# Gathered expert rows weighed and summed by the pair: one product of 2048 columns and three sums for 16 weighted additions and two copies

## The chip, the core and the metric

The kernel runs on one core of a Trainium2 chip. The core has TensorE (PE, matrix products), VectorE (DVE), ScalarE (ACT) and GpSimd (POOL), and SyncE (SP), which here only issues transfers. The metric is the device time of the program in microseconds.

## The reference

Two layers over `x`, 16 sequences of 256 tokens with 128 features. In each, `x` is normalized, a sequence operator gives `s`, an expert layer gives `g`, and `x` becomes `x + s * g`. The change is in the end of the first layer's expert part:

```
logits = x @ router_w                       # 32 experts
topk_w, topk_idx = top_k(softmax(logits), 4)
topk_w = topk_w / sum(topk_w)
combine = sum_k(one_hot(topk_idx) * topk_w)
eo = (silu(x @ w_gate[e]) * (x @ w_up[e])) @ w_down[e]      # for each expert e
routed = einsum('te,teh->th', combine, eo)
sh = (silu(x @ sh_gate) * (x @ sh_up)) @ sh_down * sigmoid(x @ sh_gate_w)
g = silu(routed + sh)
x = x + s * g
```

The kernel forms `routed + sh` for a token as the shared part plus four expert rows, each times its weight. The second layer has attention for `s` and a gated expert layer of 8 experts, and needs the first layer's `x`.

## The kernel before, in words

Every engine has a program of its own, and semaphores tie them together. A token tile is 128 tokens; a sequence `b` has two tiles, a pair `p` two sequences, that is four tiles, and there are 8 pairs. Sequences, pairs and steps are counted from 0.

**Routing and scatter.** DVE finds each token's four experts and a slot for each (`slot_of`), in two halves of 8 sequences. POOL sends each tile's normalized rows to its slots in HBM (`slot_rows`, line 553), 128 indirect transfers.

**Expert steps.** 48 steps (24 a half), each with 512 slots. SP loads the rows, TensorE turns them (L717), multiplies by the gate and up weights (L742), ScalarE takes silu (L971), DVE multiplies by the up part into `act` (`hidden`, L1322), TensorE turns `act` (L725) and multiplies by the down weights (L733), ScalarE copies the result out (L980) and SP stores it in `expert_rows`. TensorE runs the next step's gate and up product right after it has turned `act`.

**Gather.** When all rows of a half are stored, POOL fetches for each token its four result rows, `gath`, by indirect transfers (L567): one for each tile and rank, 8 a sequence, 16 a pair, in order of the sequences. The buffers are `onehot` and `route_tmp`, each with room for one pair and split in two sequences here, so that four sequences can be under way. A sequence's gathers wait until the one four before it is summed (`c_f`). All indirect transfers are issued by POOL, one behind another. Half 0's gathers (pairs 0 to 3) run beside the expert steps of half 1, those of half 1 (pairs 4 to 7) beside the second layer.

**Sum.** `sum_experts(b)` on DVE copies the sequence's eight weights to `f_w` (L1333), waits for its eight gathers (`g_in`), and adds row times weight in eight steps of 128 columns (`sum_step`, L1338), the two tiles taking turns. The first step of a tile starts from the shared part `sh_tok`. When both sequences of a pair are summed, ScalarE takes silu, and DVE does `mix` (x + s * g), `stats1`, `rstd1` and `norm1`. `rstd1` is 13 instructions on 4 columns, nearly each waiting for the one before. `rstd1(summed(b))` puts a step of a sum behind each of them (`link_beside`).

**Where the sums stand.** The order is written out by hand. In half 1's expert steps from step 29 on, five steps belong to a pair (`norm_step`): the even sequence is summed behind `hidden` of place 1, the odd one behind that of place 2, `mix` and `stats1` at place 3, `rstd1` at place 4, `norm1` at the next pair's place 0. So pairs 0 to 3 are done. For pairs 4 to 7 the table `NORM_AT` names the sequence of the second layer in which the pair is normalized: pair 4 in sequence 3, pair 5 in 5, pair 6 in 8, pair 7 in 10. `summed(b)` derives the sums from it: sequence 8 in b = 1, 9 in b = 2, 10 in b = 3 (beside `rstd1` of pair 4), 11 in b = 4, 12 in 6, 13 in 7, 14 in 8 (beside `rstd1`), 15 in 9.

**A sequence of the second layer on DVE**: row maximum (L1472), its negative (L1473), perhaps gates of the second router (L1399 to L1427), then a sum as above, the reciprocal (L1485), the product of hidden rows with spread gates (L1489), `finish` of the sequence before (L1460 to L1466), and the output weighed into `o_sb` (L1498). TensorE's scores of the next sequence (L855) wait for `o_sb`.

## Time and profile before

| | |
|---|---|
| median of 3 runs | 483.81 us (483.55 to 484.87) |
| profiled execution, device time | 484.73 us |
| its span | 483.0 us |
| mean granted TensorE clock | 0.936 |
| TensorE busy | 388.8 us (81%) |
| DVE busy | 331.8 us (69%), 1157 instructions |
| ScalarE busy | 261.0 us (54%) |
| POOL busy | 280.6 us (58%) |
| the chain that ended last | PE 36%, DVE 26%, POOL 13%, issue 11%, ACT 9%, DMA 4% |

The span is the profiled stretch, the device time has 1.7 us around it. The chain that ended last follows the program back from its end, at each step to what released it; its shares show which engines the time went through. POOL's share of it is the scatter near the beginning; the gathers come later and have no line among its largest.

### The profile page before, as it was taken

The numbers are of one execution on the slowest core, as the hardware profiler recorded it, in microseconds if no ns is written. First come the engines' busy times: TensorE is split into PE (matmuls) and PEld (weight loads), VectorE is DVE, ScalarE is ACT, GpSimd is POOL, SyncE is SP. The second block draws the span as 40 slices with busy tenths as digits, with TensorE's granted clock in tenths as the row PEclk, the third lists the DMA queues.
The fourth block names the chain that finished last, engine by engine and source line by source line (L and its number), as shares of the span: only waits on it lengthen the run. The fifth ranks groups of instructions, "written<-read, shape, count | busy, mean of one in ns | idle before, by whom it ended". The sixth has DMA issues, their size and how long they took to land.

```text
span 483.0 us, 8878 instructions
## 1 busy us (share of the span) xinstructions
PE 388.8 (81%) x2576; PEld 346.1 (72%) x2576; DVE 331.8 (69%) x1157; ACT 261.0 (54%) x497; POOL 280.6 (58%) x323
## 2 busy tenths in 40 slices
PE   0666887942499999985999999868888898898895
PEld 0665785932388888874999999757776776777774
DVE  6989887859446656640147869747998989885533
ACT  2250133400166666662666766467668675777772
POOL 6916777777777777754777777077777760000000
PEclk9997995977599999995999999899999999999998
DMA  6899991111435565635476666212222220100100
GB/s 182 268 358 305 313 401 65 52 49 49 157 132 181 197 202 193 185 127 178 154 212 206 205 210 202 99 54 67 82 77 72 72 87 8 43 24 22 45 12 22
DMA packets 48206, 67.26 MB, mean 139 GB/s; under 512 B 8842, under 2 KB 25635, under 8 KB 48163
## 3 DMA queue, kind: packets, MB, share of 16 engines
q1 hardware_dynamic: 39970, 49.93, 32.1%
q0 software_dynamic: 8192, 16.79, 11.4%
q8 instruction: 23, 0.38, 0.3%
q14 instruction: 21, 0.16, 0.1%
HBM read 28.93 MB, written 35.65 MB: 134 GB/s over the span
## 4 chain that ended last, share of the span: by engine, by line
PE 36%; DVE 26%; POOL 13%; issue 11%; ACT 9%; DMA 4%; SPq 1%; DVEq 0%; ACTq 0%; POOLq 0%
POOL slot_rows L553 13%; PE ps L742 12%; PE ps L733 5%; PE ps L717 4%; PE ps L725 3%; DMA rows<-slot_rows 3%; DVE trig L1338 3%; ACT L1099 2%; DVE mx L1472 2%; ACT sg L971 2%; PE ps L855 2%; DVE rows L1489 1%; PE ps L888 1%; PE ps L841 1%; DVE act L1322 1%
## 5 line engine op out<-in xcount | busy, mean ns | idle before, releaser
L553 POOL DMA_INDIRECT slot_rows<-xn_tok,slot_of x128 | 136.5, 1066 | 51.2 <-issue 38.7
L567 POOL DMA_INDIRECT onehot<-expert_rows,slot_of x64 | 61.5, 961 | 38.8 <-DMA expert_rows<-zeros 19.9
L1322 DVE TENSOR_TENSOR act<-sg,ps 128x384 f32<-128x384 f32 x48 | 26.6, 554 | 78.3 <-ACT sg L971 78.0
L567 POOL DMA_INDIRECT route_tmp<-expert_rows,slot_of x64 | 62.0, 969 | 19.5 <-issue 19.5
L733 PE MATMUL ps<-w_dn,actT 96*128 x384 | 51.0, 275 | 1.5 <-ACT actT L989 1.5
L733 PEld LDWEIGHTS ps<-w_dn,actT 96*128 96x128 f32 x384 | 46.8, 192 | 2.1 <-issue 2.0
L971 ACT ACTIVATE sg<-ps 128x384 f32<-128x384 f32 x48 | 23.6, 491 | 38.7 <-PE ps L742 38.6
L717 PE MATMUL ps<-ident,rows 128*128 128x128 f32 x192 | 32.2, 294 | 8.4 <-DMA rows<-slot_rows 5.9
L742 PE MATMUL ps<-w_gu,raw_fc 128*128 x192 | 37.9, 343 | 0.0
L980 ACT COPY zeros<-ps 128x512 f32<-128x512 f32 x48 | 28.2, 587 | 15.6 <-PE ps L733 15.2
L742 PE MATMUL ps<-w_gu,raw_pr 128*128 x192 | 35.6, 329 | 0.0
L717 PEld LDWEIGHTS ps<-ident,rows 128*128 128x128 f32 x192 | 24.4, 151 | 14.4 <-DMA rows<-slot_rows 8.8
L944 ACT ACTIVATE hs_t<-ps 128x512 f32<-128x512 f32 x16 | 9.6, 597 | 46.0 <-PE ps L650 46.0
L819 PE MATMUL ps<-prT,rows 128*128 128x128 f32 x256 | 33.3, 286 | 1.2 <-DVE raw_fc L1466 1.2
L819 PEld LDWEIGHTS ps<-prT,rows 128*128 128x128 f32 x256 | 31.9, 200 | 2.1 <-issue 1.3
L742 PEld LDWEIGHTS ps<-w_gu,raw_fc 128*128 128x128 f32 x192 | 33.0, 202 | 0.0
L725 PE MATMUL ps<-ident,act 128*96 128x128 f32 x192 | 30.4, 281 | 2.5 <-DVE act L1322 2.4
L1489 DVE TENSOR_TENSOR rows<-rows,ps 128x1024 f32<-128x1024 f32 x16 | 19.5, 1218 | 18.5 <-PE ps L882 9.8
L742 PEld LDWEIGHTS ps<-w_gu,raw_pr 128*128 128x128 f32 x192 | 30.6, 190 | 0.0
L861 PE MATMUL ps<-hs_t,fcT 128*128 128x256 f32 x128 | 30.2, 379 | 0.0
L888 PE MATMUL ps<-decay_t,hs_t 128*128 128x128 f32 x128 | 18.5, 288 | 13.7 <-ACT hs_t L1102 13.7
L989 ACT COPY actT<-ps 96x512 f32<-96x512 f32 x48 | 28.0, 583 | 2.9 <-PE ps L725 2.7
(223 smaller groups left out, 889.5 us busy)
## 6 DMA issues: line engine op xcount, KB each, us to landing
slot_rows<-zeros SPq DMA_DIRECT2D x12, 1024.0 KB, 12.4
rows<-slot_rows SPq DMA_DIRECT2D x48, 256.0 KB, 3.0
expert_rows<-zeros SPq DMA_DIRECT2D x48, 256.0 KB, 2.1
x_tok<-in_L_attn_x_dram SPq DMA_DIRECT2D x8, 256.0 KB, 5.7
slot_rows<-xn_tok,slot_of POOLq DMA_INDIRECT x128
hs_t<-xn_tok SPq DMA_DIRECT2D x16, 128.0 KB
out_dram<-raw_fc SPq DMA_DIRECT2D x16, 128.0 KB, 1.8
w_dn<-in_L_ffn_w_down_dram SPq DMA_DIRECT2D x1, 1536.0 KB
```

Of the source, the lines that this page charges most:

```text
L553: g.indirect_dma_start(out=slot_rows[r], out_offset=bass.IndirectOffsetOnAxis(ap=slot_of[:, n:n + 1], axis=0), in_=xn_tok[:, r * HT + t, : ...
L567: g.indirect_dma_start(out=gath[b % 4][:, j, :], out_offset=None, in_=expert_rows[r], in_offset=bass.IndirectOffsetOnAxis(ap=slot_of[:, n: ...
L717: mm = pe.transpose(ps[:, 0, j * P:(j + 1) * P], rows[slot][:, j * P:(j + 1) * P], ident[:])
L725: mm = pe.transpose(ps[0:I0, 5, j * P:(j + 1) * P], act[u][:, j, :], ident[:])
L733: mm = pe.matmul(ps[:, 6, j * P:(j + 1) * P], actT[u][:, j * P:(j + 1) * P], w_dn[:, bass.ds(e[j] * P, P)], start=True, stop=True)
L742: mm = pe.matmul(ps[:, 1 + 2 * u + j // 2, (j % 2) * 256:(j % 2) * 256 + 2 * I0], exT[u][:, j * P:(j + 1) * P], w_gu[:, bass.ds(e[j], 1), ...
L819: mm = pe.matmul(ps[:, 3, j * P:(j + 1) * P], hg[u][:, c, j * P:(j + 1) * P], prT[:, c, :], start=(c == 0), stop=(c == CH1 - 1))
L861: mm = pe.matmul(ps[:, 4 + c // 2, (c % 2) * SEQ:(c % 2 + 1) * SEQ], fcT[:, c, :], xn1T[u], start=True, stop=True)
L971: a.activation(sg[u][:].rearrange("p (a b) i -> p a b i", a=2), ps[:, 1 + 2 * u:3 + 2 * u, :].rearrange("p a (b i) -> p a b i", b=2)[:, :, ...
L980: a.copy(eo[slot], bank(6)).then_inc(e_out, 1)
L989: a.copy(actT[u][:], ps[0:I0, 5, :]).then_inc(e_aTs, 1)
L1322: v.tensor_tensor(act[u][:].rearrange("p (a b) i -> p a b i", a=2), sg[u][:].rearrange("p (a b) i -> p a b i", a=2), ps[:, 1 + 2 * u:3 + 2 ...
```

## The change

Buffers and gathers are counted by pairs: `gath` has two buffers of 16 rows a token tile group, `onehot` and `route_tmp`, there are two semaphores `g_in`, and a pair's 16 gathers wait once, for the pair two before it to be summed. `c_f` counts pairs. On DVE `weigh_rows(p)` waits for all 16 gathers of the pair and multiplies its 2048 columns in place by the weights, each spread over 128 columns. `sum_rows(p)` adds ranks 0 and 1 to 2 and 3 (1024 columns), then the shared part (512), then the other half (512). In the expert steps `weigh_rows` stands at place 1, `sum_rows` at place 2. In the second layer `weigh_rows` comes two sequences before the pair is normalized and `sum_rows` one before. `rstd1` no longer has steps of a sum between its instructions; `f_w`, the copies and `link_beside` are gone.

```diff
+def weighed(b):
+    return turned(b + 2) if b >= 0 else None
 def summed(b):
-    for ahead in (2, 1):
-        if b >= 0 and turned(b + ahead) is not None:
-            return 2 * turned(b + ahead) + 2 - ahead
-    return None
+    return turned(b + 1) if b >= 0 else None
...
-            for b in range(NSEQ):
-                r = b // (NSEQ // NH)
-                if b % (NSEQ // NH) == 0:
+            for p in range(FSEQ):
+                r = p // (FSEQ // NH)
+                if p % (FSEQ // NH) == 0:
                     for u in range(4):
                         pool.wait_ge(e_stored[u], 16 * (r + 1) * SG // 4)
-                if b >= 4:
-                    pool.wait_ge(c_f, b - 3)
-                for j in range(2 * TOP0):
-                    n = b * 2 * TOP0 + j
...
+                if p >= 2:
+                    pool.wait_ge(c_f, p - 1)
+                for j in range(GT):
+                    for k in range(TOP0):
+                        n = (p * GT + j) * TOP0 + k
+                        g.indirect_dma_start(
+                            out=gath[p % 2][:, j, k, :], out_offset=None, in_=expert_rows[r],
+                            in_offset=bass.IndirectOffsetOnAxis(ap=slot_of[:, n:n + 1], axis=0)).then_inc(g_in[p % 2], 16)
...
-                sc.wait_ge(c_f, 2 * p + 2)
+                sc.wait_ge(c_f, p + 1)
...
-            def sum_step(b, n, marks):
...
-            def sum_experts(b):
-                marks = []
-                for n in range(2 * TOP0):
-                    sum_step(b, n, marks)
+            def weigh_rows(p):
+                dve.wait_ge(g_in[p % 2], 16 * GT * TOP0 * (p // 2 + 1))
+                w = top_w[:, p * GT * TOP0:(p + 1) * GT * TOP0].rearrange("p (t k a) -> p t k a", t=GT, a=1)
+                link(v.tensor_tensor(gath[p % 2], gath[p % 2], w.to_broadcast([P, GT, TOP0, P]), ALU.mult))
+            def sum_rows(p):
+                g = gath[p % 2]
+                link(v.tensor_tensor(g[:, :, 0:2, :], g[:, :, 0:2, :], g[:, :, 2:4, :], ALU.add))
+                link(v.tensor_tensor(f_sb, g[:, :, 0, :], sh_tok[:, p * GT:(p + 1) * GT, :], ALU.add))
+                v.tensor_tensor(f_sb, f_sb, g[:, :, 1, :], ALU.add).then_inc(c_f, 1)
...
                 if step == 1:
-                    sum_experts(2 * q)
+                    weigh_rows(q)
                 if step == 2:
-                    sum_experts(2 * q + 1)
+                    sum_rows(q)
...
                 if turned(b) is not None:
-                    rstd1(summed(b))
-                elif summed(b) is not None:
-                    sum_experts(summed(b))
+                    rstd1()
+                if weighed(b) is not None:
+                    weigh_rows(weighed(b))
+                if summed(b) is not None:
+                    sum_rows(summed(b))
```

On DVE at pair 3, expert steps 45 to 47, the program before has (`act` is the step's product, `trig` the sum's buffer `f_sb`, `route_tmp` the gathered rows):

```order
L1322 TENSOR_TENSOR act<-sg,ps 128x384
L1333 COPY f_w<-top_w 128x8
L1338 SCALAR_TENSOR_TENSOR trig<-route_tmp,f_w,sh_tok 128x128 x2
L1338 SCALAR_TENSOR_TENSOR trig<-route_tmp,f_w,trig 128x128 x6
L1322 TENSOR_TENSOR act<-sg,ps 128x384
L1333 COPY f_w<-top_w 128x8
L1338 SCALAR_TENSOR_TENSOR trig<-route_tmp,f_w,sh_tok 128x128 x2
L1338 SCALAR_TENSOR_TENSOR trig<-route_tmp,f_w,trig 128x128 x6
L1322 TENSOR_TENSOR act<-sg,ps 128x384
```

And now:

```order
L1310 TENSOR_TENSOR act<-sg,ps 128x384
L1320 TENSOR_TENSOR route_tmp<-route_tmp,top_w 128x2048
L1310 TENSOR_TENSOR act<-sg,ps 128x384
L1324 TENSOR_TENSOR route_tmp<-route_tmp 128x4x256
L1325 TENSOR_TENSOR trig<-route_tmp,sh_tok 128x512
L1326 TENSOR_TENSOR trig<-trig,route_tmp 128x512
L1310 TENSOR_TENSOR act<-sg,ps 128x384
```

The whole pair is weighed where one sequence was summed, with one wait in front of it.

On DVE in sequence 1 of the second layer (from the second router's `top_i` on), the program before has:

```order
L1402 MAX_INDEX top_i<-top,lg 128x8 x8
L1405 TENSOR_TENSOR gd<-top 128x8
L1406 CAST g_f<-top_i 128x16
L1333 COPY f_w<-top_w 128x8
L1338 SCALAR_TENSOR_TENSOR trig<-onehot,f_w,sh_tok 128x128 x2
L1338 SCALAR_TENSOR_TENSOR trig<-onehot,f_w,trig 128x128 x6
L1485 RECIPROCAL rden<-den 128x2
L1489 TENSOR_TENSOR rows<-rows,ps 128x1024
```

And now:

```order
L1377 MAX_INDEX top_i<-top,lg 128x8 x8
L1380 TENSOR_TENSOR gd<-top 128x8
L1381 CAST g_f<-top_i 128x16
L1320 TENSOR_TENSOR onehot<-onehot,top_w 128x2048
L1462 RECIPROCAL rden<-den 128x2
L1466 TENSOR_TENSOR rows<-rows,ps 128x1024
```

The product of pair 4 stands ahead of the same reciprocal and the same product of hidden rows.

## Rows read from the trace of the kernel before

**Rows 1.** Stretches: busy us of PE, PEld, DVE, ACT, POOL; granted clock; DMA share; GB/s.

```profile
250.00:312.00 62.00, 58.91 (x444) 55.98 (x443) 49.57 (x208) 41.39 (x82) 40.27 (x42) 1.00 0.61 189
312.00:400.00 88.00, 73.53 (x476) 62.79 (x475) 71.83 (x285) 61.40 (x117) 62.12 (x64) 0.98 0.26 74
```

**Rows 2.** Timeline, sequence 1 of the second layer: start, us, instruction [idle before].

```profile
330.80 0.17 DVE L1333 COPY f_w<-top_w 128x8 f32<-128x8 f32 x1
331.07 1.03 ACT L1099 ACTIVATE rows<-ps 128x1024 f32<-128x1024 f32 x1
331.65 0.61 PE L882 MATMUL ps<-logits,expert_sel 24*128 24x256 bf16 x4
333.11 0.16 DVE L1485 RECIPROCAL rden<-den 128x2 f32<-128x2 f32 x1
333.30 1.22 DVE L1489 TENSOR_TENSOR rows<-rows,ps 128x1024 f32<-128x1024 f32 x1
```

**Rows 3.** Timeline of POOL, gathers of half 1: pair 4's first and last, pair 5's last.

```profile
314.56 0.95 POOL L567 DMA_INDIRECT onehot<-expert_rows,slot_of  x1 [11.79 <-DMA expert_rows<-zeros]
...
333.53 0.95 POOL L567 DMA_INDIRECT onehot<-expert_rows,slot_of  x1 [0.30 <-issue]
...
354.01 0.95 POOL L567 DMA_INDIRECT route_tmp<-expert_rows,slot_of  x1 [0.30 <-issue]
```

**Rows 4.** Timeline of POOL, half 0: the last gathers of pairs 2 and 3.

```profile
281.35 0.95 POOL L567 DMA_INDIRECT onehot<-expert_rows,slot_of  x1 [0.30 <-issue]
...
301.68 1.10 POOL L567 DMA_INDIRECT route_tmp<-expert_rows,slot_of  x1 [0.30 <-issue]
```

**Rows 5.** Timeline of DVE, pair 2's first copy and pair 3's sums.

```profile
282.75 0.17 DVE L1333 COPY f_w<-top_w 128x8 f32<-128x8 f32 x1
...
300.62 0.17 DVE L1333 COPY f_w<-top_w 128x8 f32<-128x8 f32 x1
...
303.70 0.55 DVE L1322 TENSOR_TENSOR act<-sg,ps 128x384 f32<-128x384 f32 x1 [0.69 <-ACT sg L971]
...
304.38 0.61 DVE L1338 SCALAR_TENSOR_TENSOR trig<-route_tmp,f_w,sh_tok 128x128 f32<-128x128 f32 x2
```

**Rows 6.** Groups of DVE instructions by form, 240 to 483 us: busy us, mean ns | idle before.

```profile
L1489 DVE TENSOR_TENSOR rows<-rows,ps 128x1024 f32<-128x1024 f32 x16 | 19.5, 1218 | 18.5 <-PE ps L882 9.8 <-ACT rows L1099 8.6
...
L1361 DVE TENSOR_TENSOR trig<-out_cs,xnT 128x512 f32<-128x512 f32 x4 | 2.8, 693 | 0.0
```

**Rows 7.** Timeline of DVE and POOL, two places where they overlap.

```profile
73.75 1.22 DVE L1279 TENSOR_TENSOR_SCAN rec<-decay,rec 128x512 f32<-128x512 f32 x1
73.81 1.94 POOL L553 DMA_INDIRECT slot_rows<-xn_tok,slot_of  x1 [0.30 <-issue]
...
347.04 0.69 DVE L1361 TENSOR_TENSOR trig<-trig,xnT 128x512 f32<-128x512 f32 x1
...
347.39 1.15 POOL L567 DMA_INDIRECT route_tmp<-expert_rows,slot_of  x1 [0.30 <-issue]
```

**Rows 8.** Timeline of DVE, `rstd1` alone (ahead of L1386) and with sums between (sequence 3).

```profile
311.00 0.17 DVE L1379 TENSOR_SCALAR v<-mv 128x4 f32<-128x4 f32 x1
...
313.45 1.11 DVE L1386 TENSOR_SCALAR rec<-x_tok,mv,r 128x128 f32<-128x128 f32 x4
...
350.61 0.17 DVE L1379 TENSOR_SCALAR v<-mv 128x4 f32<-128x4 f32 x1
...
354.63 0.17 DVE L1485 RECIPROCAL rden<-den 128x2 f32<-128x2 f32 x1
```

**Rows 9.** Busy by stretch as in rows 1; timeline of TensorE; chain that ended last.

```profile
220.00:223.00 3.00, 0.49 (x3) 0.49 (x4) 0.00 (x0) 0.00 (x0) 0.85 (x1) 0.50 0.88 307
...
222.51 1.12 PE L717 MATMUL ps<-ident,rows 128*128 128x128 f32 x4 [3.86 <-DMA rows<-slot_rows]
...
225.48 2.57 PE ps L742 x8
230.01 1.30 PE ps L742 x8
```

More of the change, by code:

```diff
@@ L242, in build @@
         f_act = out_cs[:].rearrange("p c (a d) -> p (c a) d", d=P)
-        f_w = [sb(f"f_w{u}", [P, 2 * TOP0]) for u in range(2)]
         st1 = sb("st1", [P, 4, 6])
@@ L331, in build @@
         e_stored = [sem(f"e_stored{u}") for u in range(4)]
-        g_in = [sem(f"g_in{u}") for u in range(4)]
+        g_in = [sem(f"g_in{u}") for u in range(2)]
         xr_in = [sem(f"xr_in{u}") for u in range(2)]
@@ L1058, in tanh_f @@
             def tanh_f(p):
-                sc.wait_ge(c_f, 2 * p + 2)
+                sc.wait_ge(c_f, p + 1)
                 a.activation(f_act, f_sb, ACT.Tanh, scale=0.5).then_inc(c_fact, 1)
@@ L1373, in stats1, with rstd1 @@
                 link(last)
[L1375 to L1380 removed]
+            def rstd1():
+                link(v.tensor_scalar(v1[:], mv1[:, :, 1], EPS, None, ALU.add))
+                rsqrt_steps(nc, link, r1[:], v1[:], t1[:])
             def norm1(p):
```

36 lines of the change are left out of this document (2 added, 34 removed).

## The prediction

> **What bounds the kernel now.** I read the page first, then busy time by stretch, then the gathers and the DVE rows around them. The chain that ended last is spread over four engines, with DVE's line 1338, the sums to be replaced, among its pieces. By stretch two regimes stand out. From 250 to 312 us, the last expert steps, TensorE is busy 58.91 of 62 us: each step begins as the one before it ends, and DVE only has to deliver `act` in time. From 312 to 400 us, attention with pairs 4 to 7 between, DVE has 71.83 of 88 us and TensorE 73.53 with pauses [rows 1]. There the chain is DVE's. In sequence 1 the gate product at 333.30 starts 0.2 us after the reciprocal, though its inputs were ready with the gelu at 332.10 and the spread gates at 332.26 [rows 2]. So DVE is already 1.0 us late there, and anything added in front of 333.11 moves the rest.
>
> The quantity that decides is when gathered rows are there. Gathers start 1.26 us apart: pair 4's first at 314.56, its sixteenth at 333.53, pair 5's sixteenth at 354.01 [rows 3]. In the first half pair 2's last one starts at 281.35, pair 3's at 301.68 [rows 4]. The landing is not shown, but bounded: pair 3's last gather leaves POOL at 302.78 and DVE uses its row at 304.38, at once after its copy [rows 4, 5]. So it is between 0 and 1.6 us; I take 1.5, because nearest to the only row.
>
> By the Trainium skill ("DMA: Bandwidth & Descriptors", Anatomy of one DMA — SWDGE (gpsimd) path) a DMA of this kind has a fixed cost of about 2.0 us. Counted from the start of the 1.10 us gather that would be 0.9 us behind its end, which agrees with the bound; each wait below would be 0.6 us shorter by it.
>
> **The change part by part.**
>
> *The arithmetic.* Removed per pair: two copies and sixteen steps of 128 columns. In sequence 1 a copy and eight steps take 330.80 to 333.11, 2.31 us [rows 2], so 4.6 us a pair. Added: products of 512 columns take 693 ns and of 1024 columns 1218 ns [rows 6], 1.025 ns a column and 168 ns fixed. The trace has none of 2048 columns; by the line it is 2.27 us, at least 1.22 (the 1024 row) and, at that row twice over, at most 2.44. I take 2.3. The three sums have 1024, 512 and 512 columns: 1.22 + 0.69 + 0.69 and two links of 0.03, 2.7 us. A pair needs 5.0 us in place of 4.6: the instructions are fewer, the columns the same, and a product and an addition that were one pass are now two.
>
> *The wait for the pair.* `weigh_rows` stands where the even sequence was summed, but waits for 16 gathers and not for 8. The eight more take 10 us of POOL. The places:
> - Pair 3: DVE comes to it at 300.62; its rows are there at 302.78 + 1.5 = 304.3. It waits 3.7, the product ends at 306.6, and the next `act` product, at 303.70 before [rows 5], is 2.9 late. TensorE's transposes of `act`, the next gate/up group and with them every later step are queued behind it, and the last stores, on which POOL's second series of gathers waits, move too.
> - Pair 2: wanted at 282.75, there at 282.30 + 1.5 = 283.8; a wait of 1.0 of which 0.7 is idle time that DVE had.
> - Pair 4, in sequence 1: wanted at 330.80, there at 333.53 + 0.95 + 1.5 = 336.0. Wait 5.2, all of it late, since the gate product, the finish, `o_sb` and TensorE's next scores are queued behind it.
> - Pairs 0, 1, 6 and 7: their rows are there first, by the same pitch.
> If the landing were 0 or 1.6, the waits of pairs 3 and 4 would be 1.5 shorter or 0.1 longer each.
>
> *POOL held up by wide DVE instructions.* A POOL issue that starts within a DVE instruction with both inputs in SBUF lasts until that ends. At 73.81, just inside the scan of 73.75 to 74.97, it takes 1.94 us; at 347.39, inside the product of 347.04 to 347.73, 1.15 [rows 7]; clear of such instructions gathers take 0.95 [rows 3]. The hold ends some 0.15 us before the DVE instruction does. The old steps hold for 0.13 us or so each. The product holds for 2.1, which is longer than the pitch of the gathers: one always starts inside it, on average 0.63 in, and is 1.5 late (least 0.9, most 2.1). The sums, holding 1.07, 0.53 and 0.53, add 0.5 + 0.1 + 0.1 on average. That is 2.2 a pair, less 0.1 for the old steps. Since pair 1's gathers run under pair 0's sums and so on, pair 2's rows come 4.2 later (288.0) and pair 3's 6.3 later (310.6). The product then ends at 312.9 and the step that began at 303.70 is 9.2 late; with the least hold it is 2.9 + 3 x 0.9 = 5.6. I take 8: nearer to the average, and a little under it because pair 0's product starts shortly before a gather ends. It takes the place of the 2.9 above.
>
> The Trainium skill ("SBUF — State Buffer", Who interferes with whom) says that a DVE instruction with two SBUF inputs contends with a GpSimd instruction that reads SBUF, whichever issued first keeping the port, but infers that descriptor generation isn't held by `tensor_tensor`. By the first rule the sum is mine; by the inference it is that of the first rival. The issues at 73.81 and 347.39 stand for the first.
>
> *Attention's sum.* Pair 4's wait 5.2. Its sums in sequence 2, in the path like those of sequence 1: 2.7 for 2.3, +0.4. Pair 5 in sequence 3: before, the steps filled the links of the reciprocal root, the two together taking 350.61 to 354.63, 4.0 us; alone the root takes 311.00 to 313.45, 2.45 us [rows 8]. With the product that is 4.75: +0.7. Pair 5's last gather, held by pair 4's product and sums (2.2), lands at 354.96 + 2.2 + 1.5 = 358.7, and DVE wants it at 350.61 + 5.2 + 0.4 + 2.45 = 358.7: +0.3, between 0 and 0.7. Pair 6 +0.4 in sequence 7, pair 7 +0.7 in sequence 8. The sums in sequences 4 and 9 stand beside ScalarE's table loads and gelu; nothing (0.4 each if that cover is gone). 5.2 + 0.4 + 0.7 + 0.3 + 0.4 + 0.7 = 7.7.
>
> *TensorE's clock.* After the pause of 3.86 us before 222.5 the granted clock was 0.50, the lower of its levels, 1.2 of 2.4 GHz, and the gate/up group took 2.57 us in place of 1.30 [rows 9]. The three waits above 3 us leave TensorE idle as long. A spell costs about 2 us in the expert steps (that group and its neighbours), next to nothing where DVE is the limit: between 0 and 6, I take 2.
>
> *POOL's own waits* for `c_f` now name a whole pair. Pair 6's gathers need pair 4 summed, one sequence (10 us) after 333.11 and 5.6 late, at 349, and follow pair 5's last at 354.01 [rows 3] anyway: nothing. The same holds for pair 7.
>
> The sum, against the profiled execution: 483.0 span and 1.7 around it are 484.73; + 8 + 7.7 + 2 = 502.4. Its 484.73 lie 0.9 above the median of 483.81, so the median should be 501.5.
>
> **The rivals.**
> 1. *Only the waits*, POOL not held. For: the issues of [rows 3] all show 0.95 us. Against: the issues at 73.81 and 347.39. Then 2.9 + 7.4 + 1 of clock = 11.3, and the median is 495.1.
> 2. *One wait covered.* Should DVE's wait in the expert steps lie beside a row load or a store that ends as late, or the landing be near 0, 5 to 8 us are left: 489 to 492. Against: `act` is what TensorE waits for at each of these steps.
> 3. *Not slower: both waits covered.* If DVE had slack behind sequence 1 of as much as 5.2 us, the wait would only take the place of idle time further on (from that slack on it decides), and the 4.6 for 5.0 us of work would be lost in it too: 484. For it speaks that DVE is idle 16 of 88 us from 312 to 400. Against: the row at 333.30 has its slack used up.
> 4. *More than counted*: every product holding for its longest and a clock spell at each wait: 9.2 + 8.5 + 6, the median at 507.5 or above.
>
> **How the numbers follow.** A difference of 0.3%, 1.5 us, is what a measurement of this kernel can tell from none. The forecast 0.54, its own range 497 to 506; rival 1 0.23; rival 2 0.08; rival 3 0.06; rival 4 0.09. The range of 8 in 10 takes in the forecast and rival 1 and leaves out rivals 2 and 3 and most of 4: 492.5 to 507.5. Slower: all but rival 3, 0.94. Rival 3 is split: 0.03 within 0.3%, 0.03 faster.
>
> **What would show it.** In the profile after: DVE idle in front of the product of 2048 columns, ended by a gather, for about 5 us each at pairs 2, 3 and 4, nothing at pairs 0, 6 and 7. The product about 2.3 us. Some POOL issue of 2 to 3 us under each product, and pair 3's last gather near 309 in place of 301.7. The second series of gathers starting near 323 in place of 314.6. Sequences 10 to 15 as long as before. I am wrong if the wait at pair 4 is under 4 us, if the product is far from 2.3, or if no POOL issue under a product is longer than 1.4 us.

## The result: 4.2% slower, and the profile after

| | before | after |
|---|---|---|
| median | 483.73 us (483.55 to 484.87, 4 runs) | 503.51 us (502.87 to 506.49, 4 runs) |
| profiled execution, its span | 484.73, 483.0 us | 504.15, 502.4 us |
| mean granted TensorE clock | 0.936 | 0.921 |
| DVE busy | 331.8 us, 1157 instructions | 334.3 us, 1045 instructions |
| POOL busy | 280.6 us | 292.7 us |

The ratio is 1.0416, with a 95% interval from 1.037 to 1.0462. The forecast was 501.5 us, within 492.5 to 507.5. The two profiled spans differ by 19.4 us.

The page of the kernel after shows where the reader has to look. Its section 4 is the chain that ended last, first by engine, then by engine, tile and line.

```profile
POOL 29%; DVE 22%; PE 20%; issue 15%; ACT 7%; DMA 6%; SPq 1%; DVEq 0%; POOLq 0%; ACTq 0%
```

Before, the chain was 36% TensorE, 26% DVE and 13% POOL, and POOL's 13% were the scatter alone. Now the gathers `onehot L555` and `route_tmp L555` have 9% and 7% of it: TensorE has lost its place to them.

By stretch, busy time of PE, PEld, DVE, ACT, POOL, then granted clock, DMA share and GB/s, the kernel after, as in [rows 1]:

```profile
250.00:312.00 62.00, 54.53 (x389) 52.12 (x388) 40.64 (x134) 36.05 (x71) 47.49 (x43) 0.92 0.58 176
312.00:400.00 88.00, 69.83 (x427) 59.78 (x426) 65.45 (x220) 53.05 (x103) 56.38 (x54) 0.92 0.24 68
```

In the same 62 us TensorE gets 4.4 us less done and DVE 8.9, while POOL is busy 7.2 us longer with as many instructions (43 for 42). Longer busy time for the same count is a sign of instructions held up, not of more work. I call it a hold when a POOL issue lasts longer than its usual 0.94 us because a DVE instruction is running.

The waits of DVE in the kernel after: who waits, for what, total us, times, the longest.

```profile
DVE onehot L1320 <- DMA onehot<-expert_rows,slot_of: 9.8, 2, 6.0
DVE route_tmp L1320 <- DMA route_tmp<-expert_rows,slot_of: 4.1, 2, 2.4
```

L1320 is the product of 2048 columns. Of its eight instances four wait for gathers, 13.9 us together. The timeline (start, us, instruction, idle before) gives their places, pairs 1 to 4: ahead of each product the pair's sixteenth gather, behind the first two also the POOL issue that runs beside them:

```profile
264.50 0.94 POOL L555 DMA_INDIRECT route_tmp<-expert_rows,slot_of  x1 [0.30 <-issue]
...
267.49 2.29 DVE L1320 TENSOR_TENSOR route_tmp<-route_tmp,top_w 128x2048 f32<-128x2048 f32 x1 [2.40 <-DMA route_tmp<-expert_rows,slot_of]
268.24 2.36 POOL L555 DMA_INDIRECT onehot<-expert_rows,slot_of  x1 [0.30 <-issue]
...
286.87 0.94 POOL L555 DMA_INDIRECT onehot<-expert_rows,slot_of  x1 [0.30 <-issue]
...
289.89 2.29 DVE L1320 TENSOR_TENSOR onehot<-onehot,top_w 128x2048 f32<-128x2048 f32 x1 [5.95 <-DMA onehot<-expert_rows,slot_of]
290.62 2.39 POOL L555 DMA_INDIRECT route_tmp<-expert_rows,slot_of  x1 [0.30 <-issue]
292.22 0.55 DVE L1310 TENSOR_TENSOR act<-sg,ps 128x384 f32<-128x384 f32 x1
...
309.35 0.94 POOL L555 DMA_INDIRECT route_tmp<-expert_rows,slot_of  x1 [0.30 <-issue]
...
312.09 2.29 DVE L1320 TENSOR_TENSOR route_tmp<-route_tmp,top_w 128x2048 f32<-128x2048 f32 x1 [1.69 <-DMA route_tmp<-expert_rows,slot_of]
314.42 0.55 DVE L1310 TENSOR_TENSOR act<-sg,ps 128x384 f32<-128x384 f32 x1
...
344.42 0.94 POOL L555 DMA_INDIRECT onehot<-expert_rows,slot_of  x1 [0.30 <-issue]
...
347.05 2.29 DVE L1320 TENSOR_TENSOR onehot<-onehot,top_w 128x2048 f32<-128x2048 f32 x1 [3.82 <-DMA onehot<-expert_rows,slot_of]
349.38 0.17 DVE L1462 RECIPROCAL rden<-den 128x2 f32<-128x2 f32 x1
```

The sixteenth gathers are those at 264.50, 286.87, 309.35 and 344.42. Those of pairs 2 and 3, at 281.35 and 301.68 before [rows 4], are 5.5 and 7.7 later. The `act` product at 303.70 before [rows 5] stands at 314.42. The reciprocal of sequence 1, at 333.11 before [rows 2], stands at 349.38, 16.3 later. POOL's second series starts 11.1 later than in [rows 3]:

```profile
325.70 0.94 POOL L555 DMA_INDIRECT onehot<-expert_rows,slot_of  x1 [15.41 <-DMA expert_rows<-zeros]
```

**Two stages.** For everything that follows I divide the program at one instruction that every kernel has: the row maximum `mx` of a sequence of the second layer. Its first (sequence 0) ends the expert stage, its last (sequence 15) the attention stage. Before, they start at 315.91 and 468.09; after, at 325.55 and 487.56. So 9.6 of the us were lost in the expert stage and 9.8 in attention. In attention the delay is 12.5 us at sequence 1, 17.2 at sequence 2, 18.6 at sequence 4, and 19.5 from sequence 9 to the end.

The delay at the last `act` product, just ahead of the first `mx`, is 10.7 (318.42 for 307.71), and so 1.1 more than at `mx`. That 1.1 us is a clock spell of the kernel before: its TensorE ran at the low level there, and takes 8.2 us from the last `act` product to `mx`; the kernel after ran that stretch at 1.00, in 7.1.

```profile
312.00:314.00 2.00, 2.00 (x7) 1.64 (x7) 1.72 (x11) 0.28 (x1) 0.00 (x0) 0.50 0.35 131
```

I call a spell a stretch of a few us at the low granted clock. Which spells an execution has differs from kernel to kernel, and each one that isn't followed by a wait for something else is worth 1 to 1.5 us in these figures.

### The profile page after: what moved, and what is told of

Read it like the earlier page. It is cut to its first block, busy times and chain, and to the rows that moved or that the text cites. A ratio compares the mean times of both kernels' runs of the same rounds, so it can differ in the third digit from the quotient of the medians.

```text
span 502.4 us, 8755 instructions
## 1 busy us (share of the span) xinstructions
PE 397.3 (79%) x2576; PEld 353.2 (70%) x2576; DVE 334.3 (67%) x1045; ACT 261.1 (52%) x497; POOL 292.7 (58%) x323
## 4 chain that ended last, share of the span: by engine, by line
POOL 29%; DVE 22%; PE 20%; issue 15%; ACT 7%; DMA 6%; SPq 1%; DVEq 0%; POOLq 0%; ACTq 0%
POOL slot_rows L540 13%; POOL onehot L555 9%; POOL route_tmp L555 7%; PE ps L730 5%; DMA rows<-slot_rows 3%; PE ps L721 2%; PE ps L849 2%; PE ps L705 2%; ACT L1087 2%; PE ps L843 1%; PE ps L807 1%; DVE rows L1466 1%; DVE route_tmp L1320 1%; DVE mx L1447 1%; PE ps L876 1%
## 5 line engine op out<-in xcount | busy, mean ns | idle before, releaser
L555 POOL DMA_INDIRECT onehot<-expert_rows,slot_of x64 | 65.6, 1025 | 42.8 <-DMA expert_rows<-zeros 24.0
L555 POOL DMA_INDIRECT route_tmp<-expert_rows,slot_of x64 | 70.3, 1098 | 21.3 <-issue 21.3
L730 PE MATMUL ps<-w_gu,raw_fc 128*128 x192 | 39.0, 350 | 0.0
L977 ACT COPY actT<-ps 96x512 f32<-96x512 f32 x48 | 28.0, 583 | 11.7 <-PE ps L713 11.6
L849 PE MATMUL ps<-hs_t,fcT 128*128 128x256 f32 x128 | 32.6, 400 | 0.0
L1466 DVE TENSOR_TENSOR rows<-rows,ps 128x1024 f32<-128x1024 f32 x16 | 19.5, 1218 | 18.5 <-PE ps L870 9.8
L713 PEld LDWEIGHTS ps<-ident,act 128*96 128x96 f32 x192 | 20.0, 127 | 14.3 <-DVE act L1310 13.0
## 6 DMA issues: line engine op xcount, KB each, us to landing
w_dn<-in_L_ffn_w_down_dram SPq DMA_DIRECT2D x1, 1536.0 KB, 16.3
```

The lines of the kernel that those rows point to most:

```text
L555: g.indirect_dma_start(out=gath[p % 2][:, j, k, :], out_offset=None, in_=expert_rows[r], in_offset=bass.IndirectOffsetOnAxis(ap=slot_of[:, ...
L713: mm = pe.transpose(ps[0:I0, 5, j * P:(j + 1) * P], act[u][:, j, :], ident[:])
L730: mm = pe.matmul(ps[:, 1 + 2 * u + j // 2, (j % 2) * 256:(j % 2) * 256 + 2 * I0], exT[u][:, j * P:(j + 1) * P], w_gu[:, bass.ds(e[j], 1), ...
L849: mm = pe.matmul(ps[:, 4 + c // 2, (c % 2) * SEQ:(c % 2 + 1) * SEQ], fcT[:, c, :], xn1T[u], start=True, stop=True)
L977: a.copy(actT[u][:], ps[0:I0, 5, :]).then_inc(e_aTs, 1)
L1466: v.tensor_tensor(hg[u], hg[u], ps[:, 0:2, :].rearrange("p a (b n) -> p (a b) n", b=2), ALU.mult).then_inc(d_hs, 1)
```

## The experiments

### Six runs beside a disturbance

The first six runs settled nothing about time. In those two sessions every engine paused now and then, the longest time in each run for 37 to 43 us, for nothing that the profile could name, and the kernel before itself took 740 us (medians 739.68 in the first four, 743.65 in the last two). A difference of 10 us can't be read beside that. The record gives chip 0 for the first session and chip 5 for the second; five of the six later runs were made on chip 5 too, and there the kernel before then took 484 to 485 us. The kernels are those of the sections below, where their edits stand, and they were run again later with the same expectations. These six, with what was on record for them:

The waits alone, measured 740.12 us, ratio 1.0042 (0.9993 to 1.009); and again, 744.46, ratio 0.9932 (0.9866 to 0.9997):

> The kernel before with one thing added: the even sequence's sum also waits for the odd one's eight gathers. Narrow steps, copies, order and POOL's waits as before. Theory: the waits without the holds. Landing 2.0 us after the issue ends: pair 2 about 1 us late, pair 3 about 3.4 us, pair 4 waits 5.5 us, and 2 to 4 us of lower clock behind them: 495 to 498; the POOL issues stay at 0.95 us. Rival (the wide instructions cost nothing of their own): as the changed kernel, 502 to 504. Rival (the wait is small, the holds are all): 485 to 488.

> The kernel before with one thing added: the even sequence's sum also waits for the odd one's eight gathers. Narrow steps, copies, order and POOL's waits as before. Theory: the waits without the holds. Landing 2.0 us after the issue ends: pair 2 about 1 us late, pair 3 about 3.4 us, pair 4 waits 5.5 us, and 2 to 4 us of lower clock behind them: 495 to 498; the POOL issues stay at 0.95 us. Rival (the wide instructions cost nothing of their own): as the changed kernel, 502 to 504. Rival (the wait is small, the holds are all): 485 to 488.

The product in eight pieces, 745.32 us, ratio 1.0102:

> The changed kernel with the product of 2048 columns cut in eight of 256, back to back, no links between. Theory (POOL waits for the one DVE instruction that it meets): holds under a product are at most 0.3 us, 0.25 a pair on average in place of 1.5; the longest POOL issue under a product is under 1.3 us; the product takes 2.7 us for 2.3; pair 3's rows come about 3.7 us earlier: 498 to 501. Rival (DVE keeps POOL out as long as its two-input instructions follow each other): POOL issues of 2 us and more remain, 503 to 505.

Half waits, 743.93 us, ratio 1.0083 (1.004 to 1.0127):

> The changed kernel, with four semaphores for the gathers, so that DVE waits for the even sequence's eight gathers where the product stood and for the odd one's where the sums stand; the product is two of 1024 columns. Theory (pair wait, POOL held up, clock): the wait of sequence 1 of the second layer goes, since pair 4's second eight are asked for 10 us later; in the expert steps holds of 0.5 and 0.5 for the products and 0.7 for the sums, 1.7 us a pair, still put pair 3's last gather near 307.8, landed near 309.8, so that DVE waits there about 5 us for the odd half; the work at that place is 3.9 us in place of 2.4. Median 491 to 496. Rival (the wait for the whole pair is all): 484 to 487.

TensorE kept busy, 744.80 us, ratio 1.0105 (1.0016 to 1.0193); and again, 745.53, ratio 1.0035:

> The changed kernel with small unused TensorE products (128x64, bf16, into columns that are overwritten later) where TensorE would be idle: 80 and 30 in the waits of pairs 2 and 3, 36 in sequence 0 and 80 ahead of the scores of sequence 2 of the second layer. Theory (part of the loss is the lower granted clock after the waits): the granted clock stays at 1.00 from 286 to 360 us, the step that took 6.5 us behind pair 2's wait takes 4.0 again, and the time falls by 4 to 7 us, to 497 to 500. Rival (the lower clock costs nothing where DVE is waited for): 502 to 505.

> The changed kernel with small unused TensorE products (128x64, bf16, into columns that are overwritten later) where TensorE would be idle: 80 and 30 in the waits of pairs 2 and 3, 36 in sequence 0 and 80 ahead of the scores of sequence 2 of the second layer. Theory (part of the loss is the lower granted clock after the waits): the granted clock stays at 1.00 from 286 to 360 us, the step that took 6.5 us behind pair 2's wait takes 4.0 again, and the time falls by 4 to 7 us, to 497 to 500. Rival (the lower clock costs nothing where DVE is waited for): 502 to 505.

One thing could be read in them, since it is a single instruction's length: with the whole product POOL's longest gather issue was 2.48 and 2.49 us, with the product in pieces 1.42.

### Only the waits

The kernel before, in which an even sequence's sum also waits for the gathers of the odd one. Nothing is added on DVE, and no instruction is wide.

```diff
                     dve.wait_ge(g_in[b % 4], 16 * 2 * TOP0 * (b // 4 + 1))
+                    if b % 2 == 0:
+                        dve.wait_ge(g_in[b % 4 + 1], 16 * 2 * TOP0 * (b // 4 + 1))
```

> The kernel before with one thing added: the even sequence's sum also waits for the odd one's eight gathers. Narrow steps, copies, order and POOL's waits as before. Theory: the waits without the holds. Landing 2.0 us after the issue ends: pair 2 about 1 us late, pair 3 about 3.4 us, pair 4 waits 5.5 us, and 2 to 4 us of lower clock behind them: 495 to 498; the POOL issues stay at 0.95 us. Rival (the wide instructions cost nothing of their own): as the changed kernel, 502 to 504. Rival (the wait is small, the holds are all): 485 to 488.

Measured: 494.81 us against 485.35 for the kernel before in the same session, ratio 1.0173 (1.0099 to 1.0247), that is 8.4 us, or 9.5 by the medians. That is 0.2 below the expected 495 to 498, and far from both rivals. DVE's rows in front of the sum (L1340 here) at pairs 2, 3 and 4:

```profile
286.17 0.67 DVE L1340 SCALAR_TENSOR_TENSOR trig<-onehot,f_w,sh_tok 128x128 f32<-128x128 f32 x2 [3.98 <-DMA onehot<-expert_rows,slot_of]
...
305.13 0.61 DVE L1340 SCALAR_TENSOR_TENSOR trig<-route_tmp,f_w,sh_tok 128x128 f32<-128x128 f32 x2 [0.52 <-DMA route_tmp<-expert_rows,slot_of]
...
340.84 0.61 DVE L1340 SCALAR_TENSOR_TENSOR trig<-onehot,f_w,sh_tok 128x128 f32<-128x128 f32 x2 [3.77 <-DMA onehot<-expert_rows,slot_of]
```

and its gathers by group (count, busy us, mean ns, idle before), first of this kernel, then of the kernel after:

```profile
L567 POOL DMA_INDIRECT route_tmp<-expert_rows,slot_of x64 | 61.8, 965 | 19.5 <-issue 19.5
L567 POOL DMA_INDIRECT onehot<-expert_rows,slot_of x64 | 61.7, 965 | 45.2 <-DMA expert_rows<-zeros 26.3 <-issue 18.9
```

```profile
L555 POOL DMA_INDIRECT onehot<-expert_rows,slot_of x64 | 65.6, 1025 | 42.8 <-DMA expert_rows<-zeros 24.0 <-issue 18.9
L555 POOL DMA_INDIRECT route_tmp<-expert_rows,slot_of x64 | 70.3, 1098 | 21.3 <-issue 21.3
```

With the wait alone a gather takes 965 ns as ever. With the change the 128 gathers take 12.4 us more of POOL (135.9 for 123.5). The wait by itself costs about half of the whole loss. Where it does: the first `mx` is 3.5 us late for 9.6 with the whole change, and the rest of the expert stage's loss needs the wide instructions. Attention takes 161.0 us in place of 152.2. Not all of these 8.9 us are the wait's: 1.5 of them come in sequence 4 (11.9 us for 10.4 in the kernels before and after), where this execution's granted clock was 0.55 from 376 to 379 and those two have no spell.

```profile
370.05 0.68 DVE L1474 TENSOR_REDUCE mx<-ps 128x2 f32<-128x512 f32 x1
...
381.96 0.69 DVE L1474 TENSOR_REDUCE mx<-ps 128x2 f32<-128x512 f32 x1 [1.34 <-PE ps L855]
```

Without that spell the wait accounts for some 7.3 of attention's 9.8 us. One profiled execution doesn't tell whether the spell belongs to this kernel or to the execution.

### The product in eight pieces

The kernel after, with the product of 2048 columns issued as eight of 256.

```diff
-                link(v.tensor_tensor(gath[p % 2], gath[p % 2], w.to_broadcast([P, GT, TOP0, P]), ALU.mult))
+                for t in range(GT):
+                    for k in (0, 2):
+                        g = gath[p % 2][:, t:t + 1, k:k + 2, :]
+                        last = v.tensor_tensor(g, g, w[:, t:t + 1, k:k + 2, :].to_broadcast([P, 1, 2, P]), ALU.mult)
+                link(last)
```

> The changed kernel with the product of 2048 columns cut in eight of 256, back to back, no links between. Theory (POOL waits for the one DVE instruction that it meets): holds under a product are at most 0.3 us, 0.25 a pair on average in place of 1.5; the longest POOL issue under a product is under 1.3 us; the product takes 2.7 us for 2.3; pair 3's rows come about 3.7 us earlier: 498 to 501. Rival (DVE keeps POOL out as long as its two-input instructions follow each other): POOL issues of 2 us and more remain, 503 to 505.

Measured: 500.05 us against 483.71, ratio 1.0333 (1.0266 to 1.04), as expected: 16.3 us slower than before in place of 19.8, though DVE now spends half a us more on each product. The two intervals just meet (the change's begins at 1.037), so by the times alone the gain is likely and not certain; the rows show the hold itself. DVE and POOL at pair 2:

```profile
285.66 2.77 DVE L1323 TENSOR_TENSOR onehot<-onehot,top_w 128x256 f32<-128x256 f32 x8 [2.09 <-DMA onehot<-expert_rows,slot_of]
286.50 1.07 POOL L555 DMA_INDIRECT route_tmp<-expert_rows,slot_of  x1 [0.30 <-issue]
287.88 1.04 POOL L555 DMA_INDIRECT route_tmp<-expert_rows,slot_of  x1 [0.30 <-issue]
...
288.94 1.22 DVE L1328 TENSOR_TENSOR onehot<-onehot 128x1024 f32<-128x1024 f32 x1
...
289.22 1.76 POOL L555 DMA_INDIRECT route_tmp<-expert_rows,slot_of  x1 [0.30 <-issue]
```

The same two operands, the same buffer and the same number of columns: under one instruction of 2.29 us an issue takes 2.39, under eight short ones 1.07 and 1.04. What decides how long POOL is held is the length of the single DVE instruction. The sum of 1024 columns, left whole, still stretches the issue at 289.22 to 1.76 us. Pair 3's last gather starts at 304.30 in place of 309.35, and the first `mx` is 5.2 us later than before instead of 9.6. In attention nothing is won back (163.9 us, 1.9 more than after): the wait at pair 4 is as long (3.78), and each of the four products there costs DVE 0.5 more.

### A wait and a product for each half of a pair

The kernel after with four semaphores. The product of the first half stands where the whole one stood, the second half's directly ahead of the sums. The sums are as in the kernel after.

```diff
-            def weigh_rows(p):
-                dve.wait_ge(g_in[p % 2], 16 * GT * TOP0 * (p // 2 + 1))
-                w = top_w[:, p * GT * TOP0:(p + 1) * GT * TOP0].rearrange("p (t k a) -> p t k a", t=GT, a=1)
-                link(v.tensor_tensor(gath[p % 2], gath[p % 2], w.to_broadcast([P, GT, TOP0, P]), ALU.mult))
+            def weigh_rows(p, h=0):
+                dve.wait_ge(g_in[2 * (p % 2) + h], 16 * 2 * TOP0 * (p // 2 + 1))
+                b, g = 2 * p + h, gath[p % 2][:, 2 * h:2 * h + 2, :, :]
+                w = top_w[:, b * 2 * TOP0:(b + 1) * 2 * TOP0].rearrange("p (t k a) -> p t k a", t=2, a=1)
+                link(v.tensor_tensor(g, g, w.to_broadcast([P, 2, TOP0, P]), ALU.mult))
             def sum_rows(p):
+                weigh_rows(p, 1)
```

> The changed kernel, with four semaphores for the gathers, so that DVE waits for the even sequence's eight gathers where the product stood and for the odd one's where the sums stand; the product is two of 1024 columns. Theory (pair wait, POOL held up, clock): the wait of sequence 1 of the second layer goes, since pair 4's second eight are asked for 10 us later; in the expert steps holds of 0.5 and 0.5 for the products and 0.7 for the sums, 1.7 us a pair, still put pair 3's last gather near 307.8, landed near 309.8, so that DVE waits there about 5 us for the odd half; the work at that place is 3.9 us in place of 2.4. Median 491 to 496. Rival (the wait for the whole pair is all): 484 to 487.

Measured: 489.55 us against 483.71, ratio 1.0108 (1.0052 to 1.0164), 5.8 us slower by the medians (5.2 by the ratio) and below the expected 491 to 496. The wait that was expected for the odd half at pair 3 did not occur: no row of DVE waits for a gather in this kernel.

```profile
303.33 0.94 POOL L555 DMA_INDIRECT route_tmp<-expert_rows,slot_of  x1 [0.30 <-issue]
...
303.57 0.56 DVE L1310 TENSOR_TENSOR act<-sg,ps 128x384 f32<-128x384 f32 x1
304.04 1.22 DVE L1321 TENSOR_TENSOR route_tmp<-route_tmp,top_w 128x1024 f32<-128x1024 f32 x1
```

Behind the `act` product of 303.57 the first half's product of pair 3 starts at once. This is the kernel after with nearly all of its arithmetic, and 14 of its 19.8 us are gone. What is left, 5.8 us, I put down to the second pass over the columns and the shorter holds, without having divided it.

### TensorE kept busy in the waits, twice

The clock term was to be tested by products without a use, placed where TensorE would wait (the first with 80, 30, 36 and 80 of them in front of pair 2's and pair 3's turn of `act` and in sequences 0 and 2; the second with 160, 30, 36 and 185). The diff is that of the second; the 36 of sequence 0 are left out of it.

```diff
+            def idle_products(count, bank):
+                for _ in range(count):
+                    pe.matmul(ps[:, bank, 448:512], ident_bf[:], ident_bf[:, 0:64], start=True, stop=True)
...
+                idle = {(2, 2): 160, (3, 2): 30}.get(norm_step(n), 0)
+                if idle:
+                    pe.wait_ge(e_aTs, n)
+                    idle_products(idle, 5)
                 act_T(n, n % 2, n == 0)
...
+                if b == 2:
+                    idle_products(185, 2)
                 if b:
                     pe.wait_ge(d_os, b)
```

> The changed kernel with small unused TensorE products (128x64, bf16, into columns that are overwritten later) where TensorE would be idle: 80 and 30 in the waits of pairs 2 and 3, 36 in sequence 0 and 80 ahead of the scores of sequence 2 of the second layer. Theory (part of the loss is the lower granted clock after the waits): the granted clock stays at 1.00 from 286 to 360 us, the step that took 6.5 us behind pair 2's wait takes 4.0 again, and the time falls by 4 to 7 us, to 497 to 500. Rival (the lower clock costs nothing where DVE is waited for): 502 to 505.

Measured: 505.93 us against 483.71, ratio 1.046 (1.0406 to 1.0513). The expectation failed. The clock did stay up in the middle of three places, but the 80 products took only some 2.5 us and did not fill the other two:

```profile
290.00:296.00 6.00, 4.56 (x19) 4.54 (x20) 3.87 (x5) 0.77 (x2) 5.08 (x4) 0.63 0.19 54
330.00:342.00 12.00, 10.59 (x103) 9.57 (x102) 4.68 (x31) 9.82 (x19) 9.16 (x10) 1.00 0.22 55
350.00:356.00 6.00, 5.21 (x12) 4.21 (x13) 3.59 (x15) 2.15 (x5) 4.78 (x5) 0.50 0.34 98
```

With the full clock from 330 to 342, sequence 0's `mx` to sequence 1's took 12.2 us, for 14.7 in the kernel after. Little of the 2.5 was kept (from the first `mx` to the third it is 28.7 us for 29.3): DVE came to the product of pair 4 earlier and waited longer.

```profile
345.21 2.29 DVE L1333 TENSOR_TENSOR onehot<-onehot,top_w 128x2048 f32<-128x2048 f32 x1 [5.85 <-DMA onehot<-expert_rows,slot_of]
```

Its wait is 5.85 us, for 3.82 after. So I formed a second view, that the clock hardly matters where a wait on POOL stands behind, and put in enough products to fill the two places.

> As the run with small unused TensorE products, but enough of them to fill the waits: 160 behind pair 2 (80 took 2.5 us of 5.3) and 185 ahead of sequence 2's scores (80 took 2.5 of 6.6). New theory: what ends pair 3's wait and pair 4's is POOL's gathers, so a lower clock in front of them only shortens those waits; with the clock kept, pair 3's wait grows from 1.7 to about 5 us and its product starts no earlier against the last gather, and only the spell behind pair 4's wait is won: 1 to 2 us below the changed kernel, 501.5 to 502.5. Rival (each spell costs what it lengthens): 4 to 7 us below, 496.5 to 499.5. Rival (the clock falls nonetheless): 503 to 506.

Measured: 503.27 us against 484.24, ratio 1.0402 (1.035 to 1.0454). Against 1.0416 for the change itself that is no difference that can be measured, and 503.27 is above the 501.5 to 502.5 of my theory, in the range of the last rival. The clock was full at both places, and no longer at others; in the middle row, behind the expert steps, it is 0.83, where the kernel after has 1.00:

```profile
280.00:300.00 20.00, 20.00 (x281) 19.55 (x280) 10.52 (x30) 10.49 (x21) 15.43 (x15) 1.00 0.59 182
320.00:330.00 10.00, 7.67 (x32) 5.85 (x32) 7.85 (x38) 4.90 (x11) 3.09 (x4) 0.83 0.19 66
342.00:362.00 20.00, 18.02 (x270) 16.04 (x268) 13.19 (x31) 10.66 (x21) 15.43 (x15) 1.00 0.23 64
```

One gain is visible in the trace and small. The scores of sequence 2, first in the kernel after, then in this one:

```profile
352.72 2.05 PE L843 MATMUL ps<-hs_h 128*128 128x256 f32 x4 [4.81 <-DVE o_sb L1475]
```

```profile
352.98 1.13 PE L854 MATMUL ps<-hs_h 128*128 128x256 f32 x4 [0.19 <-DVE o_sb L1488]
```

From the reciprocal of sequence 1 to the row maximum of sequence 2 it is 4.4 us here (349.73 to 354.14), 5.4 in the kernel after (349.38 to 354.80) and 4.5 before. That is 1 us won.

This run doesn't settle what the clock is worth in the total, for three reasons. Its products at pair 2 ended late: TensorE was in them until 296.96, and the transposes of `act`, which was ready at 295.05, came 1.7 us late, so that the step took 5.7 us where 4.0 were wanted. New spells came: at pair 1, where the clock fell behind a wait and the step took 6.1 us for 4.0; from 322 to 327, where it is 8.2 us from the last `act` product to `mx` for 7.1; and in sequence 4, 11.4 us for 10.4, with 0.59 from 381 to 384. The last two have no wait for POOL close behind, and the one in sequence 4 takes back the 1 us won in sequence 2. And the wait at pair 3, which the theory wanted at about 5 us, was 1.88. What both runs do show is one place, the wait at pair 4: the two times that TensorE kept its clock in sequence 0, that wait grew from 3.82 to 5.85 and 5.01 us.

### Without the copies of the weights

The kernel before with `f_w` and its 16 copies taken out, `top_w` read instead: the one part of the change that removes work.

> The kernel before without the copies of the weights: each narrow step takes its weight from the routing table itself. Theory: DVE is the limit in sequences 1, 2, 3, 6, 7 and 8 of the second layer, and a copy with its link takes 0.2 us there (0.4 where it runs into a POOL issue); six of them are 1.2 to 1.6 us, the others stand beside waits: 1 to 2 us below the kernel before, 482 to 483. Rival (the copies lie beside other waits): no change within 0.5 us. Rival (a weight read from a column of a wide table is slower than from a copy): 1 us above.

Measured: 483.40 us (12 runs) against 483.71 (16 runs), ratio 0.9984 (0.9951 to 1.0017). The gain, if there is one, is below what 12 runs can show. Attention takes 152.1 us for 152.2, but that is no proof that the copies are worth nothing: sequence 6 takes 11.0 us for 9.8, with the granted clock at 0.56 from 386 to 389 where the kernel before has 1.00, and the other sequences together are 1.2 us shorter, 1.0 of it in sequences 1, 2 and 3. The theory's 1 to 2 us may well be there, hidden by a spell; the runs leave it open. This profiled execution is a warning, too: its first `mx` is 2.7 us later than in the kernel before, for a program that does the same there. Single executions differ that much in the expert stage, so my figures for that stage are good to 2 or 3 us, and those for attention to 1 or 2, a spell or two.

### The stages side by side

From the timelines, one profiled execution each; us against the kernel before, and the ratio of the runs:

| kernel | expert stage | attention | ratio |
|---|---|---|---|
| after | +9.6 | +9.8 | 1.042 |
| waits alone | +3.5 | +8.9 | 1.017 |
| product in pieces | +5.2 | +11.7 | 1.033 |
| half waits | +3.8 | +4.0 | 1.011 |
| TensorE busy, 80 | +8.3 | +9.3 | 1.046 |
| TensorE busy, 160 and 185 | +11.6 | +8.0 | 1.040 |
| no copies | +2.7 | -0.1 | 0.998 |

The two stages don't add up to the ratio exactly: each is one execution, and behind the last `mx` come 13.3 us in some executions and 14.9 in others. In the attention column, a spell of waits alone (1.5 us), one of TensorE busy with 160 and 185 (1.1) and one of no copies (1.2) are contained, each at a place where the kernels before and after have none.

## Why the prediction was right, and which terms were off

**The mechanism held.** The eight added gathers are waited for at pairs 2, 3 and 4, and POOL is held under the wide instructions. Rival 1, waits alone without the hold, gave 495.1 as its time; the experiment that makes it true took 494.8, in a session where the kernel before took 1.6 more than where the change was timed. It is refuted as an account of this change by the POOL issues of 2.36 and 2.39 us and by the ratio, 1.0173 (1.0099 to 1.0247) for 1.0416 (1.037 to 1.0462). Rivals 2 and 3, one or both waits covered, fall too: with the waits alone the program is 1.7% slower, and attention has no slack of 5 us, since a delay of 16.3 us at the reciprocal was never given back. Rival 4 is only half wrong. Its two stage terms, 9.2 and 8.5, were reached and passed (10.7 and 8.8); its 6 of clock are what did not come. Its sum had an error, too: with every product holding for its longest, 2.1 us, and not the average 1.5, the expert term would have been 11.0 and not 9.2.

**One sign of being wrong did appear.** I wrote that I am wrong if the wait at pair 4 is under 4 us. It is 3.82. By lateness the wait is what I had priced: the reciprocal of sequence 1 is 16.3 late and the second series of gathers 11.1, which leaves 5.1 for the 5.2 predicted. But the sign named the wait that the profile shows, and that one is 1.3 shorter, since DVE came to pair 4 12.4 us late and POOL 11.1. DVE was 9.7 late at the reciprocal of sequence 0 (328.60 for 318.89); the rest came in sequence 0, where the clock spell from 334 to 341 lies. The sign was badly chosen, and the mechanism behind it stands on the 11.1 and the 16.3.

**Prices that came out.** The product takes 2.29 us (2298 and 2292 ns on the mean of four) for the 2.27 of the line through [rows 6]. The sums take 1218, 691 and 691 ns. Pair 3's last gather starts at 309.35, "near 309". The second series of gathers starts at 325.70, later than my "near 323". Sequences 10 to 15 are as long as before, since the delay stays at 19.5. Pairs 0, 5, 6 and 7 wait for nothing; for pair 5 I had 0.3.

**The expert term: 8 predicted, 10.7 measured** at the `act` product of 303.70 (314.42 after). Three steps of that sum were off, and they add up:
- The landing. I took 1.5 us behind the end of a gather, held under 1.6 by the one place that showed it [rows 4, 5]. From the ends of the last gathers to the products that waited for them it is 2.05, 2.08, 1.80 and 1.69 us at pairs 1 to 4. For pair 3 that is 0.3 too little. One gather that landed within 1.6 bounded itself and no other; the range should have reached beyond it.
- POOL's delay. Its last gather of pair 3 was to be 6.3 late and is 7.7: the first gather of all starts 0.7 later than in the kernel before (222.87 for 222.15), and pair 0's product and sums delay the gathers by 2.7 in place of 2.1, since its sum of 1024 columns stretched a gather to 1.80 us. Pairs 1 and 2 delay them by 2.1 each, as predicted. Less the 0.16 by which this last gather itself is shorter than the one in [rows 4], these two points make 9.2 + 0.3 + 1.4 - 0.2 = 10.7.
- The rounding down to 8. I chose 8 below an average of 9.2, on the argument that pair 0's product starts shortly before a gather ends. It did, but that places the next issue early in the product, at 249.14, 0.55 us behind its start, and that one took 2.55 us. The argument pointed the wrong way and cost 1.2 us.

**Pair 1, where no wait was predicted.** I compared pair 1 by the pitch alone and left out my own term, that pair 0's instructions hold its gathers. They are 3.4 late (264.50), and DVE waits 2.4. By the rows it cost little in the end, since the product of pair 3 starts when POOL has delivered, and DVE was waiting there still.

**The visible waits.** I wrote "about 5 us each at pairs 2, 3 and 4". They are 5.95, 1.69 and 3.82. What was wrong was the picture and less the lateness: by pair 3 DVE was already 9.7 us late (309.85 for 300.15), so little was left to wait for. A wait in a profile tells how early the waiting engine came, not how much the other engine delays the program.

**The clock: 2 predicted, about 1 found, and a rest left open.** From 250 us on, three spells of the low level came in the kernel after and stood there in none before, and the one of the kernel before at 312 was gone. The first spell by stretch, the kernel after, columns as above:

```profile
289.00:292.00 3.00, 0.00 (x0) 0.00 (x0) 2.11 (x1) 0.00 (x0) 2.39 (x3) 0.68 0.71 220
292.00:295.00 3.00, 2.17 (x11) 2.15 (x12) 2.90 (x5) 0.58 (x1) 2.42 (x2) 0.50 0.08 22
295.00:298.00 3.00, 3.00 (x11) 2.91 (x12) 0.36 (x1) 0.19 (x1) 2.36 (x3) 0.50 0.17 44
```

TensorE had done nothing from 289 to 292, and the granted clock fell to 0.50, 1.2 of 2.4 GHz. The step from 292.22 to the next `act` product at 298.75 took 6.5 us, for 4.0 before. But behind it stands the product of 312.09, whose time POOL sets, and it still waits 1.69: a step 2.5 us faster would, by these rows, have waited 4.2. That is argued and not shown, since neither run with added products gave this step its 4.0 us back. The second spell, 334 to 341, stands ahead of pair 4's product in the same way, and there the run with 5.85 shows it. Only the third, 352 to 358, has no such wait behind it, and costs 0.9 us against the kernel before. I had priced the spell where TensorE is slow, and not at the next place where all engines meet.

**Attention: 7.7 predicted, 8.8 measured** beyond the expert stage's 10.7. The wait of 5.2 measured 5.1. Of the rest, 0.4 appears between the last `act` product and the second series, 0.9 is the third clock spell, which I had in the clock term, and 2.3 from sequence 2 to 9 answer to the 2.5 of sums, roots and waits that I had priced from [rows 2, 8]. The wait alone seems to cost attention 8.9 of 9.8, but 1.5 of that is a clock spell; less it, 7.3. That leaves about 2.4 for the wide instructions, near the 2.3 above. What the 4.0 of the half waits consist of I leave open.

By these figures: 10.7 + 8.8, against 8 + 7.7 + 2 = 17.7 for the forecast. Two terms were too small by 3.8 together, and of the 2 for the clock 0.9 stands inside the 8.8. The total, 501.5 for 503.5, came closer than its parts because errors of opposite sign met: that much of it is luck.

**The hold and the landing.** The rows at 268.24 and 290.62, and the pieces, show POOL's indirect issue held by a `tensor_tensor` with two inputs in SBUF. By the Trainium skill ("SBUF — State Buffer", Who interferes with whom) such an instruction contends with a GpSimd instruction that reads SBUF, and the rows agree. The same section of the Trainium skill infers that descriptor generation isn't held by `tensor_tensor`. For these gathers, which read their indices from `slot_of` in SBUF, the rows decide against it: 2.36 us under the product, 0.94 clear of it. By the Trainium skill ("DMA: Bandwidth & Descriptors", Anatomy of one DMA — SWDGE (gpsimd) path) a DMA of this kind has a fixed cost of about 2.0 us. Measured from the end of the issue on POOL to the product that waited it is 1.69 to 2.08 us, from the start of the issue 2.63 to 3.02; the figure agrees if it is counted from the end, and I had counted it from the start.

## What to carry to other kernels

Fusing small steps into one wide instruction changes three things beside the count: what it waits for (all inputs instead of the first), how long it holds up another engine's DMA issues that meet it, and how many passes the columns make; fewer instructions paid for none of them here. The half waits gave back 14 of 19.8 us with nearly the same arithmetic. Where one engine feeds another at a fixed pitch, ask for the granularity of the wait first, and keep the instructions that run beside its issues shorter than one issue. Price every delay, a slow clock too, at the next place where the engines meet: what lies ahead of a wait for a slower feeder costs nothing until the wait is used up. And before a difference of 1 us between two profiles is put down to an edit, look at the granted clock of the stretch in both.

## What the runs showed that was not expected

- Executions of one kernel lie up to 6 us apart (481.1 to 487.5 for most of 16 runs of the kernel before), and a part of that stands at the very end. From the last `mx` to the end of the span it is 14.9 us in the kernel before (468.09 to 483.0) and 13.3 in the run with 160 and 185 products (487.71 to 501.0). Some 8 us behind that `mx` TensorE runs at a mean granted clock of 0.66 in the first and of 1.00 in the second, which is done sooner. One row of each:

```profile
476.00:480.00 4.00, 2.90 (x14) 2.62 (x13) 0.62 (x2) 0.38 (x1) 0.00 (x0) 0.66 0.11 33
```

```profile
496.00:499.00 3.00, 0.89 (x8) 0.70 (x7) 1.27 (x3) 0.38 (x1) 0.00 (x0) 1.00 0.04 13
```

- Two sessions in which the kernel before took 740 us for 484, one of them under the chip number of most later runs. The chain that ended last there gave 27 to 38% of the span to "another core or an unknown queue". The waits alone came to 1.004 and 0.993 there, with narrow intervals, against 1.017 later: the difference was hidden and not only blurred.
- How regular the hold is. Each POOL issue that started inside a product ended 0.82 or 0.83 us behind it, wherever it had started: at pairs 0, 1, 2, 4, 5 and 6 the issues of 249.14, 268.24, 290.62, 348.17, 371.07 and 401.83 took 2.55, 2.36, 2.39, 2.00, 2.90 and 1.90 us. An issue clear of such instructions takes 0.94, so nearly all of it runs after the product. The longest is the one that started soonest behind the product's beginning (0.22 us, pair 5):

```profile
370.85 2.29 DVE L1320 TENSOR_TENSOR route_tmp<-route_tmp,top_w 128x2048 f32<-128x2048 f32 x1
...
371.07 2.90 POOL L555 DMA_INDIRECT onehot<-expert_rows,slot_of  x1 [0.30 <-issue]
```
